# A graph layer on one core: every third front eviction on VectorE, a node layer in three products of the sums, in the output's column order, contiguous columns in the last stage

## What is computed

```python
h = max(layernorm(x), 0)                    # x: [12500, 128]
x_s, x_v = h[:, :32], h[:, 32:].reshape(N, 32, 3)
sc_s, sc_v = x_s @ sc_ws * a / sqrt(32), einsum('nim,io->nom', x_v, sc_wv) * a / sqrt(32)
l1_s, l1_v = the same with lin1_ws, lin1_wv
weight = silu(silu(rbf(dist) @ fc_w1) @ fc_w2) @ fc_w3        # per edge, four parts of 32
gs, gv = l1_s[src], l1_v[src]                                 # the gather
msg_s = concat(w00 * gs * sh0, w11 * dot(gv, sh1) / sqrt(3))              # 64
msg_v = concat(w01 * gs * sh1, w10 * gv * sh0)                            # 64 x 3
agg_s, agg_v = segment_sum(msg_s, dst) / cnt, segment_sum(msg_v, dst) / cnt
l2_s, l2_v = agg_s @ lin2_ws * a / 8, einsum('nim,io->nom', agg_v, lin2_wv) * a / 8
alpha = tanh(agg_s @ alpha_w * a / 8)
out = x + concat(sc_s + alpha * l2_s, (sc_v + alpha * l2_v).reshape(N, 96))
```

## Time and profile before

| | |
|---|---|
| median of 3 runs | 2078.52 us |
| the profiled execution | 2077.13 us, span 2075.2 us |
| TensorE matmul busy | 1791.7 us, 86% |
| VectorE busy | 1660.9 us, 80% |
| GpSimd busy | 1517.7 us, 73% |
| ScalarE busy | 1121.9 us, 54% |
| mean granted TensorE clock | 0.91 |
| DMA | 142.05 MB, mean 68 GB/s |

### The profile page before, as it was taken

One profiled execution on the slowest core, in us unless ns is written; L12 is line 12 of the kernel. 1 busy time (PEld: TensorE's weight loads), 2 busy tenths in 40 slices (PEclk: granted clock), 3 DMA queues, 4 the chain that ended last, 5 costly groups with the idle time before them and its releaser, 6 DMA issues. The chain is left out here.

```text
span 2075.2 us, 42789 instructions
## 1 busy us (share of the span) xinstructions
PE 1791.7 (86%) x9991; PEld 1217.4 (59%) x9991; DVE 1660.9 (80%) x4500; ACT 1121.9 (54%) x3242; POOL 1517.7 (73%) x1619
## 2 busy tenths in 40 slices
PE   6599989988998898889888888898988898889883
PEld 6466666666665666556556555565655555556552
DVE  8688888878888888878777877877787878788877
ACT  6565655555555656544444555454545544555545
POOL 5577777777777777777777777777777777777770
PEclk9799999999999989999899989989998999998996
DMA  7433232323223232222222222222222222222224
GB/s 220 110 70 66 64 69 66 69 64 68 66 63 68 66 70 63 60 56 60 58 59 56 59 59 57 58 59 58 57 59 59 58 58 59 59 58 58 59 59 131
DMA packets 334451, 142.05 MB, mean 68 GB/s; under 512 B 249827, under 2 KB 308892, under 8 KB 334428
## 3 DMA queue, kind: packets, MB, share of 16 engines
q0 software_dynamic: 50016, 102.51, 18.9%
q1 hardware_dynamic: 284412, 39.28, 11.6%
HBM read 127.87 MB, written 13.75 MB: 68 GB/s over the span
## 5 line engine op out<-in xcount | busy, mean ns | idle before, releaser
L795 POOL DMA_INDIRECT lin_g<-lin_table,src_ix x1563 | 1482.3, 948 | 486.7 <-issue 476.0
L965 ACT ACTIVATE lin_sh<-lin_g,meta 128x128 f32<-128x128 f32 x1563 | 484.4, 389 | 197.6 <-DMA lin_g<-lin_table,src_ix 196.9
L840 PE MATMUL ps_w<-w,h 128*128 128x256 f32 x1566 | 488.9, 457 | 5.9 <-DVE msg L1169 3.3
L852 PE MATMUL ps_near<-msg,onehot 128*64 128x257 f32 x3126 | 423.3, 407 | 0.0
L1138 DVE TENSOR_TENSOR lin_sh<-lin_g,ps_meta 128x576 f32<-128x576 f32 (+1 forms) x261 | 196.4, 753 | 278.1 <-DMA lin_g<-lin_table,src_ix 277.4
L840 PEld LDWEIGHTS ps_w<-w,h 128*128 128x128 f32 x1566 | 374.1, 272 | 51.0 <-ACT h L954 11.4
L864 PE MATMUL ps_sums<-far_hot,near_sums 128*128 128x128 f32 x1044 | 203.8, 323 | 204.8 <-DVE agg L1196 204.1
L864 PEld LDWEIGHTS ps_sums<-far_hot,near_sums 128*128 128x128 f32 x1044 | 153.2, 211 | 366.0 <-issue 365.1
L852 PEld LDWEIGHTS ps_near<-msg,onehot 128*64 128x64 f32 x3126 | 213.2, 145 | 180.8 <-issue 110.2
L820 PE MATMUL ps_h<-rbf,w 32*128 32x192 f32 x1044 | 240.0, 349 | 18.6 <-DVE rbf L1125 18.0
L947 ACT ACTIVATE h<-ps_h 128x384 f32<-128x384 f32 x261 | 127.8, 490 | 214.4 <-PE ps_h L820 214.1
(11 more groups left out here) (150 smaller groups left out, 1905.4 us busy)
## 6 DMA issues: line engine op xcount, KB each, us to landing
lin_g<-lin_table,src_ix POOLq DMA_INDIRECT x1563
dist_in<-in_edge_weight SPq DMA_DIRECT2D x67, 96.0 KB
xq<-in_x SPq DMA_DIRECT2D x24, 256.0 KB, 3.6
lin_table<-lin_out SPq DMA_DIRECT2D x24, 256.0 KB, 3.0
x_in<-in_x SPq DMA_DIRECT2D x24, 256.0 KB
out_dram<-skip SPq DMA_DIRECT2D x24, 256.0 KB
src_ix<-in_src SPq DMA_DIRECT2D x268, 3.0 KB, 4.4
meta<-in_edge_attr SPq DMA_DIRECT2D x264, 12.0 KB
```

The lines of the kernel that those rows point to most:

```text
L795: pool.indirect_dma_start(lin_g[rows, u, t, :], None, lin_table, bass.IndirectOffsetOnAxis(ap=src_ix[rows, u, col:col + 1], axis=0)).then_ ...
L840: mm = pe.matmul(ps_w[:, 2 * j * P:(2 * j + 2) * P], cols[:, j, :], w3[:], start=True, stop=True)
L852: mm = pe.matmul(ps_near[half * NEAR:(half + 1) * NEAR, 0:MSG + 1], onehot[:, u % 2, t, :], msg[:, u % 2, t, :], start=(j == 0), stop=(j = ...
L965: last = act.activation(lin_sh0[:, u % 2, j, :], lin_g[:, u, j, :], ACT.Copy, scale=meta[:, u, harm_col(j):harm_col(j) + 1])
```

## The change

It has three parts.

1. The front: `by_dve(n)` picks steps 2, 5, 8, ... 23. ScalarE skips their `evacuate`; VectorE does `evict(n)`, one tensor_tensor of 128x512 that multiplies psN with the row's scale, broadcast over the columns, and waits for the product, the scale and a free buffer of lin_out. It stands in VectorE's step n + 3, behind the means and the scale (and ahead of a `windows`); that of step 23 stands behind the loop of steps, ahead of `places()`. The stores and `product` wait on the semaphore of the engine that did the step.
2. The node layer has four products in place of three: the count, alpha and the scalar part (33 columns), component 0 of the vector part (32 columns), and components 1 and 2 (64 columns). The last two write PSUM with a stride of three elements, and the last reads its weights with the component innermost. `agg` so holds the output's column order.
3. The last stage: `by_parts` and `in_parts` are gone, each VectorE operation is one over contiguous columns, and `BY_ACT` goes from 3 to 2: ScalarE does two of a step's four blocks, VectorE the other two and the addition of two.

```diff
@@ -215,6 +215,7 @@
             attr_zeroed, weights_zeroed, filled, shaped, iotas = (
                 sem("attr_zeroed"), sem("weights_zeroed"), sem("filled"), sem("shaped"), sem("iotas"))
             mean_kept = sem("mean_kept")
+            evicted_dve = sem("evicted_dve")
             agg_zero, windows_set = sem("agg_zero"), sem("windows_set")
             bn_done, mean_ready, std_ready, rstd_ready, scale_set = (
                 sem("bn_done"), sem("mean_ready"), sem("std_ready"), sem("rstd_ready"), sem("scale_set"))
@@ -230,6 +231,16 @@
             PIECES = 16
             PAIRS_1 = -(-(STEPS + 1) // 2)
 
+            def by_dve(n):
+
+                return n % 3 == 2 and 0 <= n < STEPS
+
+            def wait_evicted(eng, n):
+
+                if n >= 0:
+                    mine = sum(by_dve(k) for k in range(n + 1))
+                    eng.wait_ge(evicted_dve if by_dve(n) else evacuated, mine if by_dve(n) else n + 1 - mine)
+
             def pair_cols(m):
 
                 return slice(2 * m * NB, min(2 * (m + 1) * NB, NBLK))
@@ -245,7 +256,7 @@
                                 sp.dma_start(xq[0:REST_ROWS[r], n % XB, r], rest_rows(x, r)).then_inc(x_in[n % XB], 16)
 
                     def store(n):
-                        sp.wait_ge(evacuated, n + 1)
+                        wait_evicted(sp, n)
                         if n < STEPS:
                             sp.dma_start(node_rows(lin_table, n), lin_out[:, n % OB]).then_inc(lin_stored[n % OB], 16)
                         else:
@@ -372,7 +383,8 @@
                         if n % 2 == 0 and n // 2 + 1 < PAIRS_1:
                             sqrt(n // 2 + 1)
                         copy_hT(n + 1)
-                        evacuate(n)
+                        if not by_dve(n):
+                            evacuate(n)
                         if n in (3, 5, 7):
                             b, rows = (n - 3) // 2, group_blocks()[(n - 3) // 2][1]
                             act.wait_ge(dst_in[b], 16)
@@ -390,7 +402,7 @@
 
                     def product(n):
                         pe.wait_ge(hT_ready, n + 1)
-                        at_least(pe, evacuated, n - 1)
+                        wait_evicted(pe, n - 2)
                         for k in range(blocks(n)):
                             last = pe.matmul(psN[:, n % 2, k, :], hT[:, n % HB, k * P:(k + 1) * P], w_lin1[:], start=True, stop=True)
                         last.then_inc(lin_done, 1)
@@ -449,6 +461,14 @@
 
                         dve.wait_ge(rstd_ready, m + 1)
                         dve.tensor_tensor(row_scale[:, pair_cols(m)], rstd[:, pair_cols(m)], attr_lin[:, pair_cols(m)], ALU.mult).then_inc(scale_set, 1)
+
+                    def evict(n):
+
+                        dve.wait_ge(lin_done, n + 1)
+                        dve.wait_ge(scale_set, n // 2 + 1)
+                        at_least(dve, lin_stored[n % OB], 16 * (n // OB))
+                        scaling = row_scale[:, n * NB:(n + 1) * NB].unsqueeze(2).to_broadcast([P, NB, DIM])
+                        dve.tensor_tensor(lin_out[:, n % OB], psN[:, n % 2], scaling, ALU.mult).then_inc(evicted_dve, 1)
 
                     def windows(b):
 
@@ -536,6 +556,8 @@
                         means(n)
                         if n % 2 == 0:
                             scale(n // 2 - 1)
+                        if by_dve(n - 3):
+                            evict(n - 3)
                         if n == 8:
                             dve.tensor_copy(iota1[:], iota_i[:]).then_inc(const_step, 1)
                             dve.wait_ge(const_step, 2)
@@ -549,6 +571,9 @@
                             widest_span()
                     factor(PAIRS_1 - 1)
                     scale(PAIRS_1 - 1)
+                    for n in range(STEPS - 2, STEPS):
+                        if by_dve(n):
+                            evict(n)
                     places()
                     near_turns()
                     dve.wait_ge(mean_ready, STEPS + 1)
@@ -614,6 +639,7 @@
             ps_k, ps_quot = ps_meta[:, SLOTS * META:SLOTS * META + SEG], ps_meta[:, 512 - SEG:]
             assert SLOTS * META + 2 * SEG <= 512
             ps_l2 = ps_sums[:, MSG:MSG + COLS]
+            l2_vec = ps_l2[:, 1 + MUL:COUNT].rearrange("p (c m) -> p c m", m=3)
 
             key_step = sem("key_step")
             key_out = [sem(f"key_out{b}") for b in range(GB)]
@@ -870,8 +896,10 @@
                             pe.wait_ge(sumT_ready, n + 1)
                             pe.wait_ge(agg_ready, n + 1)
                             pe.matmul(ps_l2[:, COUNT:COLS], far_hot[:, u, :], near_sums[:, u % 2, MSG:], start=True, stop=True)
-                            pe.matmul(ps_l2[:, 0:1 + HID], sumT[:, u % 2, 0:P], w_lin2[:, 0, :], start=True, stop=True)
-                            pe.matmul(ps_l2[:, 1 + HID:COUNT], sumT[:, u % 2, P:], w_lin2[:, 1, 0:HID], start=True, stop=True).then_inc(l2_ready, 1)
+                            pe.matmul(ps_l2[:, 0:1 + MUL], sumT[:, u % 2, 0:P], w_lin2[:, 0, 0:1 + MUL], start=True, stop=True)
+                            pe.matmul(l2_vec[:, :, 0:1], sumT[:, u % 2, 0:P], w_lin2[:, 0, 1 + MUL:].unsqueeze(2), start=True, stop=True)
+                            pe.matmul(l2_vec[:, :, 1:3], sumT[:, u % 2, P:], w_lin2[:, 1, 0:HID].rearrange("p (m c) -> p c m", m=2),
+                                      start=True, stop=True).then_inc(l2_ready, 1)
 
                         def turn_rows(i):
 
@@ -1252,7 +1280,7 @@
             def sem(name):
                 return st.enter_context(nc.semaphore(name))
 
-            BY_ACT = 3
+            BY_ACT = 2
             count = s3("count", [P, NBLK])
             inv = s3("inv", [P, NBLK])
             scale = s3("scale", [P, NBLK])
@@ -1267,18 +1295,6 @@
 
             whole = agg[:, 0:NBLK * COLS].rearrange("p (b c) -> p b c", c=COLS)
             result = skip[:].rearrange("p (b c) -> p b c", c=DIM)
-
-            def by_parts(t):
-
-                if len(t.shape) == 2:
-                    return t[:, 0:MUL], t[:, MUL:].rearrange("p (m c) -> p m c", m=3)
-                return t[:, :, 0:MUL], t[:, :, MUL:].rearrange("p b (m c) -> p b m c", m=3)
-
-            def in_parts(t):
-
-                if len(t.shape) == 2:
-                    return t[:, 0:MUL], t[:, MUL:].rearrange("p (c m) -> p m c", m=3)
-                return t[:, :, 0:MUL], t[:, :, MUL:].rearrange("p b (c m) -> p b m c", m=3)
 
             with nc.Block() as block:
                 @block.sync
@@ -1306,15 +1322,12 @@
                     for n in range(STEPS + 1):
                         for j in range(BY_ACT if n < STEPS else 0, blocks(n)):
                             blk, rows = n * NB + j, slice(0, P if n < STEPS else REST_ROWS[j])
-                            for part in range(2):
-                                last = dve.scalar_tensor_tensor(out=in_parts(result[rows, blk, :])[part], in0=by_parts(whole[rows, blk, 1:COUNT])[part],
-                                                                scalar=gain[rows, blk:blk + 1], in1=in_parts(result[rows, blk, :])[part],
-                                                                op0=ALU.mult, op1=ALU.add)
+                            last = dve.scalar_tensor_tensor(out=result[rows, blk, :], in0=whole[rows, blk, 1:COUNT], scalar=gain[rows, blk:blk + 1],
+                                                            in1=result[rows, blk, :], op0=ALU.mult, op1=ALU.add)
                         if n < STEPS:
                             rows = result[:, n * NB:n * NB + BY_ACT, :]
                             dve.wait_ge(grown_ready, n + 1)
-                            for part in range(2):
-                                last = dve.tensor_tensor(in_parts(rows)[part], by_parts(grown[:, n % 2])[part], in_parts(rows)[part], ALU.add)
+                            last = dve.tensor_tensor(rows, grown[:, n % 2], rows, ALU.add)
                         last.then_inc(new_ready, 1)
 
                 @block.scalar
```

## The result

The change made the kernel 0.21% slower: 2082.07 us median of 20 runs (2078.61 to 2086.9) against 2077.51 of 20 runs of the kernel before beside them (2075.11 to 2080.9), ratio 1.0021, 95% interval 1.0016 to 1.0027. The forecast was 2078.9, 0.4 us over before, with a range of 2073.5 to 2084. The time lies in the range; the difference of 4.6 us lies just beyond the 0.2% (4.2 us) that the forecast counted as none.

A forecast was written before the change was run, and what follows sets the result against it. GpSimd's gathers were taken to set the loop's pace. Front +3.5, loop 0, tail +1.1 and last stage -4.2 us sum to +0.4, so 2078.9 us, with a range of 2073.5 to 2084.

The forecast's parts named there:

- What bounds the kernel: GpSimd's gathers, 1.253 us apart, set the loop's pace; other engines matter only if GpSimd must wait for a buffer.
- The loop: One more product in each of 261 groups, 63 us of TensorE's time, was to cost 0.
- the sign of being right: From the first gather's start to the end, 2.5 to 4 us less than before.
- the rivals: Front doesn't lose: 2073.9 us, chance 0.20; stores stay at 250 GB/s: 2083.5, 0.15; TensorE bounds the loop: 2136, 0.03.
- rival 3: TensorE becomes the loop's bound once added products exceed 0.78 us per group; 2136 us at 1.0 us; chance 0.03.
- The front: Before the first gather, VectorE's evictions wait for products and delay the loop's start: +3.5 us, ends -2.8 and +6.
- The cover: From 45 us on in the front, VectorE's 8.2 us of idleness waiting for the root would absorb eviction waits.
- The 1.8 us at eviction 11: In the front, VectorE reaches this eviction at 36.14 us and waits 1.8 us for product 11.
- eviction 14: In the front, its wait was expected to find cover; a case without cover belonged to the +6 us end.
- The tail: After the last gather, five node layers with an added product of 0.24 us each: +1.1 us, ends 0.5 and 2.5.
- The last stage: Contiguous VectorE steps of 0.886 us instead of 1.05, then stores limiting at 290 GB/s: -4.2 us, ends -0.6 and -5.1.
- The sum: Whole kernel: 3.5 + 0 + 1.1 - 4.2 = +0.4 us, giving a median of 2078.9 us.

The follow-up runs named there:

- e_psum: The changed kernel with ScalarE scaling the shortcut in PSUM, the skip sum reading it there and TensorE's wait moved to skip_ready: 2076.92 us.
- e_before_psum: The kernel before with only the skip sum's source moved to PSUM (same edit, wait included): 2074.71 us, ratio 0.9987.
- e_nofront: The changed kernel with the front of before, so ScalarE evicts every step: 2088.23 us, ratio 1.0052.
- e_front: The kernel before with the change's front alone, node layer and last stage as before: 2085.34 us, ratio 1.0037.
- e_extra: The kernel before with the node layer's last product issued twice, contiguous: 2091.54 us, ratio 1.0064.
- e_extra_wait: The kernel before with the doubled product, skip sum still from SBUF, and TensorE's wait ahead of its ps_skip transposes moved to skip_ready: 2084.58 us, ratio 1.0039.
- e_two_psum: The kernel before with two accumulating products over all 129 columns, the change's last stage and the skip sum's source in PSUM: 2069.72 us, ratio 0.9965.

## Where the prediction was right, and where it was wrong

**What bounds the kernel: right.** GpSimd sets the pace throughout the loop.

**The loop: the step that failed.** "TensorE waits 203 us for VectorE in the loop, and GpSimd's buffers are released long before it asks (it waited once). Cost: 0." The premises hold: GpSimd still waits for w_s once, TensorE's wait for VectorE falls from 203 to 160.4 us (toward 140 was expected), and the strided columns cost too little to matter. What is wrong is the rule behind it, that in the loop nothing on another engine matters unless GpSimd has to wait. A gather can be stretched by what VectorE does at that moment, with no wait in the records. The page of before had a sign of it, in gathers of 1274 ns beside a median of 945; the prediction took the mean distance of 1.253 us as a constant. In the profiles the loop lost 5.4 us, which is more than the 4.6 us of the whole result; from the first gather to the end it took 3.9 us more, where 2.5 to 4 less was the sign of being right. None of the rivals names this. That the time still lies in the range is luck: the range's slow side was there with other mechanisms, and rival 3's place (TensorE's 0.78 us of slack per group) was never reached.

The Trainium skill has the mechanism: SBUF — State Buffer, section "Who interferes with whom", says that a VectorE instruction with two SBUF inputs contends with a GpSimd instruction that reads SBUF, and that one with at most one SBUF input, outside VectorE's 2-port modes, doesn't. The traces agree, 30.6 us over 103 meetings against nothing over 106.

**The front: right in mechanism, its size between 1.2 and 3.0 us where 3.5 was forecast.** "Product 23 comes 2.6 to 4.1 us later": it came 1.3 later (its group starts at 63.04 us against 61.74), and VectorE was done at 69.73 against the 68.8 plus 3.3 of the working. The loop began 1.6 us later than in the profile of before, since the barrier wait shrank from 2.30 to 1.02 us. But one profile is a poor witness here: with the old front the nine profiles have the first gather at 66.7 to 70.7 us (mean 68.7), with the new one four at 71.4 to 72.3 (mean 71.7). By those means the front costs 3.0 us, by the one clean pair of medians 1.2. The cover was real: VectorE's waits for the root fell from 11.4 to 2.3 us, against 10.6 us of new waits for products. But these lay elsewhere than worked out. The 1.8 us at eviction 11 were 0.85, the dearest wait was eviction 14's with 2.85, which was to find cover, and eviction 2 waited 2.08 us, for which the working has no term.

**The tail: right.** +1.1 forecast. The two profiles differ by 2.1, but over seven with the third product and seven without it the means are 18.8 and 17.5 us: +1.2. The added product cost 0.22 to 0.23 us where 0.24 was taken. Of the warning that non-contiguous PSUM patterns significantly slow matmuls (the Trainium skill, same page, "Door 1: The DMA port swizzle") the trace shows nothing at 32 columns (0.22 us), and at 64 no more than 0.35 us against 0.32.

**The last stage: right, 0.5 us off.** -4.2 forecast, -3.7 measured, in every kernel that has it (27.8 or 27.9 us against 31.4 or 31.5). VectorE was better than worked out (0.86 against 0.886 us), and it brought nothing, since the stores were late next, as forecast: 285 GB/s where 290 was taken. 24 x (1.05 - 0.92) + 0.63 = 3.75.

**The sum.** Without the loop's term the forecast of +0.4 stands, if the front is taken at the means: 3.0 + 1.2 - 3.7 = +0.5. With a PSUM skip sum on both sides the change costs 2.2 us by the medians (2076.92 - 2074.71), 1.5 by the ratios. That is still above +0.5: the traced loop of e_psum is 3.7 us longer than that of e_before_psum, without any loss to the skip sum.

Open: why the first gather's time differs by 4 us between profiles of kernels with the same front, why e_nofront has one run of 2078 among five of 2087 to 2091, the way by which a late product reaches VectorE's order, step by step, and how much of the edit's effect is the moved wait. That the untraced slower runs of e_nofront, e_front, e_extra and e_extra_wait lose by the same meetings is inferred, not shown.

## What to carry to other kernels

Where GpSimd sets the pace, don't ask only whether it waits: list the durations of its own instructions, and look at what VectorE does during the long ones. A VectorE operation with two SBUF sources next to them is a lottery on phase, and any edit elsewhere draws again; give it a PSUM source where you can, and the edits come nearer to costing what they cost. An eviction moved to an engine with slack still waits in that engine's order: place it so late that its product is surely done.

## What the runs showed of the hardware

- An indirect gather of 0.945 us on GpSimd that started 0.05 to 0.60 us into a VectorE tensor_tensor of 128x512 from two SBUF sources was longer by 0.56 us minus that offset, to 0.04 us, in 88 of 103 cases, and by 0.16 to 0.17 us more in 15 (the longest took 1.59 us). Beside the same operation with a PSUM source it took 0.94 us. The operation took 0.68 us in either form, and a gather that was already running when it started lost nothing (101 cases).
- A two-pass product of 32 columns written to PSUM with a stride of three elements took 0.22 us from its start to the next, a contiguous one of 33 columns 0.23. With 64 columns, and the weights read with a stride too, it took 0.35 us, the contiguous one 0.32.
- Two accumulating products of 129 columns were no dearer for the loop than two of 65 and 64: stretch minus excess 1951.0 us and 1950.4 (e_two_psum and e_before_psum).
- Stores of 256 KiB went at 285 GB/s with a DMA share of 1.02, when VectorE had the next one ready every 0.86 us.
